# Neighbouring tokens on a partition in both q, k, v stages, and the expert choice packed by TensorE

## Time and profile before

| what | value |
|---|---|
| median of 3 runs | 3302.39 us (3301.63 to 3307.78) |
| profiled execution, its own time | 3321.07 us |
| span of the profiled execution | 3319.4 us |
| TensorE busy / VectorE / ScalarE / GpSimd | 86% / 66% / 48% / 22% |
| mean granted TensorE clock | 0.908 |
| DMA | 489.03 MB, 147 GB/s over the span |
| stages, us from the start | q, k, v 0; softmax attention 228; routing 1124; experts 1397; linear q, k, v 1722; linear attention 2010; last MLP 2335 |

### The profile page before, as it was taken

One profiled execution on the slowest core, in us unless ns is written; L12 is line 12 of the kernel. 1 busy time (PEld: TensorE's weight loads), 2 busy tenths in 40 slices (PEclk: granted clock), 3 DMA queues, 4 the chain that ended last, 5 costly groups with the idle time before them and its releaser, 6 DMA issues. The chain is left out here.

```text
span 3319.4 us, 59131 instructions
## 1 busy us (share of the span) xinstructions
PE 2858.0 (86%) x19969; PEld 2057.9 (62%) x19969; DVE 2207.0 (66%) x6121; ACT 1602.5 (48%) x2398; POOL 730.4 (22%) x877
## 2 busy tenths in 40 slices
PE   7849999999999577578856777999399999999998
PEld 6734444444444266467755564556288888888887
DVE  5548999999999278593327773434466666666664
ACT  3313777777777444343315553445244444444443
POOL 0021222222222133236754431222000000000000
PEclk9877999999999766689988997889699999999999
DMA  7996656666664278647868986543343434333241
GB/s 199 254 200 90 115 112 105 111 113 112 114 112 84 89 251 288 213 159 205 220 163 249 299 267 221 172 152 114 126 110 81 96 96 89 102 82 109 74 98 45
DMA packets 429959, 489.03 MB, mean 147 GB/s; under 512 B 92880, under 2 KB 310000, under 8 KB 429552
## 3 DMA queue, kind: packets, MB, share of 16 engines
q1 hardware_dynamic: 419072, 470.52, 55.3%
q0 software_dynamic: 10240, 14.16, 2.4%
q10 hardware_dynamic: 496, 2.42, 0.3%
HBM read 280.34 MB, written 206.10 MB: 147 GB/s over the span
## 5 line engine op out<-in xcount | busy, mean ns | idle before, releaser
L545 ACT ACTIVATE att_pr<-att_e_ps 128x1024 f32<-128x1024 f32 (+2 forms) x640 | 567.2, 938 | 202.2 <-PE att_e_ps L597 202.2
L573 PE MATMUL att_m_ps<-att_ks,att_qs 63*128 63x512 f32 (+3 forms) x1536 | 465.7, 433 | 46.7 <-PEq L39 38.3
L507 DVE CUSTOM_DVE_ANT_0 att_kept<-att_m_ps,att_causal 128x256 f32<-128x256 f32 (+3 forms) x1024 | 448.5, 488 | 47.9 <-DVEq L39 21.9
L573 PEld LDWEIGHTS att_m_ps<-att_ks,att_qs 63*128 63x128 f32 x1536 | 234.1, 189 | 376.8 <-DVE att_mx L510 148.4
L510 DVE TENSOR_REDUCE att_mx<-att_m_ps 128x1 f32<-128x512 f32 x512 | 323.4, 684 | 21.4 <-PE att_m_ps L573 17.4
L486 POOL TENSOR_SCALAR_AFFINE_SELECT att_pr<-att_pr 128x256 f32<-128x256 f32 (+1 forms) x384 | 181.2, 484 | 695.8 <-PEq L588 692.2
L617 PE MATMUL att_o_ps<-att_pr,att_vs 128*32 128x512 f32 (+3 forms) x3072 | 328.9, 501 | 3.0 <-ACT att_pr L545 1.6
L2587 ACT ACTIVATE fin_hh<-fin_hid 128x512 fp32r<-128x512 f32 x192 | 121.4, 632 | 397.9 <-DVE fin_hid L2433 300.0
L597 PE MATMUL att_e_ps<-att_qs,att_ks 64*128 64x512 f32 (+3 forms) x1536 | 269.2, 376 | 5.8 <-ACT att_pr L545 3.2
L2326 POOL TENSOR_TENSOR fin_rs<-fin_ve,fin_mhalf 128x4 f32<-128x4 f32 x48 | 48.4, 1007 | 927.5 <-POOLq L39 927.5
L2429 DVE TENSOR_TENSOR fin_hid<-fin_gate,fin_u_ps 128x512 f32<-128x512 f32 x192 | 131.7, 686 | 136.4 <-ACT fin_gate L2581 82.6
(11 more groups left out here) (332 smaller groups left out, 6905.0 us busy)
## 6 DMA issues: line engine op xcount, KB each, us to landing
fin_raw<-weights SPq DMA_DIRECT2D x32, 1024.0 KB, 14.1
att_qs<-q_high SPq DMA_DIRECT2D x128, 128.0 KB, 5.0
att_ks<-k_high SPq DMA_DIRECT2D x128, 128.0 KB, 6.6
attended<-att_ot SPq DMA_DIRECT2D x64, 256.0 KB
acc<-att_zero SPq DMA_DIRECT2D x64, 256.0 KB, 2.2
moe_w<-w SPq DMA_DIRECT2D x128, 128.0 KB
lqk_a<-acc SPq DMA_DIRECT2D x32, 512.0 KB
attended<-lin_ot SPq DMA_DIRECT2D x32, 512.0 KB, 3.5
```

The costliest lines, as they stand in the source:

```text
L507: e.tensor_tensor_reduce(kept[:, n % MBUF, 0:w], m_ps[:, n % MBUF, 0:w], causal[:, BLK - w:], 1.0, -3e38, ALU.add, ALU.max, mx[:, h, at, q ...
L545: e.activation(out, src, ACT.Exp).then_inc(exp_done, 1)
L573: e.matmul(m_ps[:, (2 * i + n) % MBUF, 0:w], qs[rows, j, p, q * P:(q + 1) * P], ks[rows, j, p, h * BLK:h * BLK + w], start=True, stop=True ...
```

## The change

In both q, k, v stages, four neighbouring tokens lie on one partition: token 4p + t of the block is on partition p at place t. A partition's part of a load or store is then one piece (x 4 KB, v of softmax attention 1088 B, v of linear attention 2176 B, rows of k 2 KB). The columns of the transposed x come in the order t, p; q and k (and the features, in the linear stage) are put back in order of tokens as they are read from PSUM, with a step of 128 elements between neighbours. v's copy in the first stage is made in four instructions, v's sum in the linear stage in two, and their DMAs are joined to one. The transposes of k read its features at a step of four elements. What lies in DRAM is as before.

In the routing stage, the four transposes are replaced by four products of the mask with a 128x32 matrix `digits` of 8, 4, 2, 1, made by GpSimd at the start of the stage: the result holds for each expert and four neighbouring tokens one number. `chosen` is 64 by 2048. In the expert stage the three packing steps of VectorE go, `pack` stands ahead of the first `split`, and SyncE waits for the choice and the first weight before it issues the second weight and the second block, and for the first block before the experts' weights.

```diff
@@ phase_qkv
-        vo = ph.sb("vo", [P, 2, TPB, NH, VW])
+        vo = ph.sb("vo", [P, 2, NG, TPB, GH * VW])
-        x_v = x_d.rearrange("(b j t p) c -> b j p t c", j=2, t=TPB, p=P)
-        v_v = v_d.rearrange("(b g j t p) c -> b j t p g c", b=B, g=NG, j=2, t=TPB, p=P)
+        x_v = x_d.rearrange("(b j p t) c -> b j p (t c)", j=2, t=TPB, p=P)
+        v_v = v_d.rearrange("(b g j p t) c -> b j p g (t c)", b=B, g=NG, j=2, t=TPB, p=P)
+        def in_order(a):
+            return a.rearrange("p (t q) -> p q t", t=TPB)
-                        for t in range(TPB):
-                            e.dma_start(v_v[b[0], j, t], vo[:, j, t].rearrange("p (g h) d -> p g (h d)", g=NG)
-                                        ).then_inc(stored[j], 16)
+                        e.dma_start(v_v[b[0], j], vo[:, j].rearrange("p g t c -> p g (t c)")).then_inc(stored[j], 16)
-                            e.tensor_tensor(ol[:, j, c], qk[:, c], oh[:, j, c].bitcast(fp32),
+                            e.tensor_tensor(ol[:, j, c].rearrange("p (q t) -> p q t", t=TPB), in_order(qk[:, c]),
+                                            oh[:, j, c].bitcast(fp32).rearrange("p (q t) -> p q t", t=TPB),
-                            e.activation(oh[:, j, c], qk[:, c], ACT.Copy).then_inc(oh_ready, 1)
+                            e.activation(oh[:, j, c].rearrange("p (q t) -> p q t", t=TPB), in_order(qk[:, c]), ACT.Copy).then_inc(oh_ready, 1)
-                        e.activation(vo[:, j, :, :, 0:HD], vp[:].rearrange("p t (h d) -> p t h d", d=HD), ACT.Copy
-                                     ).then_inc(vo_ready, 1)
+                        for t in range(TPB):
+                            i = e.activation(vo[:, j, :, t].rearrange("p g (h d) -> p g h d", d=VW)[:, :, :, 0:HD],
+                                             vp[:, t].rearrange("p (g h d) -> p g h d", g=NG, d=HD), ACT.Copy)
+                        i.then_inc(vo_ready, 1)
@@ phase_project_route
-        rt = ph.sb("rt", [E, 2, BLK])
+        rt = ph.sb("rt", [E, 2, BLK // PACK])
+                step(e.memset(digits[:], 0.0))
+                for n in range(PACK):
+                    step(e.affine_select(out=digits[:], in_=digits[:], compare_op=ALU.not_equal,
+                                         fill=float(2 ** (PACK - 1 - n)), base=-n, pattern=[[-PACK, P // PACK]],
+                                         channel_multiplier=1))
-                            i = e.transpose(r_ps[:, t * P:(t + 1) * P], mask[:, t], ident[:])
+                            cols = slice(t * (P // PACK), (t + 1) * (P // PACK))
+                            i = e.matmul(r_ps[:, cols], mask[:, t], digits[:], start=True, stop=True)
@@ phase_shared_and_experts
                 load(0)
+                e.wait_ge(choice_loaded, 32)
+                e.wait_ge(w_loaded[0], 16)
                 e.dma_start(w2f[:], s2_d).then_inc(w_loaded[1], 16)
                 load(1)
+                e.wait_ge(loaded[0], 32)
                 for n in range(SETS):
                     load_experts(n)
-                    member = chosen[:].rearrange("p (g i) -> p g i", i=PACK)
-                    step(e.scalar_tensor_tensor(bits[:], member[:, :, 0], 2.0, member[:, :, 1], ALU.mult, ALU.add))
-                    for i in range(2, PACK):
-                        step(e.scalar_tensor_tensor(bits[:], bits[:], 2.0, member[:, :, i], ALU.mult, ALU.add))
-                split(0, w1h, w1l, w1f)
                 e.wait_ge(choice_loaded, 32)
                 e.wait_ge(iotas_ready, 2)
                 pack()
+                split(0, w1h, w1l, w1f)
                 split(1, w2h, w2l, w2f)
-                    e.dma_start(chosen[i * E0:(i + 1) * E0], mt_d[:, i * HALF:(i + 1) * HALF]).then_inc(choice_loaded, 16)
+                    e.dma_start(bits[i * E0:(i + 1) * E0], mt_d[:, i * GROUPS:(i + 1) * GROUPS]).then_inc(choice_loaded, 16)
@@ phase_linear_qkv
-            return d.rearrange("(b j t p) c -> b j p t c", j=2, t=TPB, p=P)
+            return d.rearrange("(b j p t) c -> b j p (t c)", j=2, t=TPB, p=P)
-        kt_v = fkt_d.rearrange("(b f j t p) c -> b j f p t c", b=B, f=2, j=2, t=TPB)
-        v_v = v_d.rearrange("(b f j t p) c -> b j f p t c", b=B, f=2, j=2, t=TPB)
+        kt_v = fkt_d.rearrange("(b f j p t) c -> b j p f (t c)", b=B, f=2, j=2, t=TPB)
+        v_v = v_d.rearrange("(b f j p t) c -> b j p f (t c)", b=B, f=2, j=2, t=TPB)
-                                e.scalar_tensor_tensor(phi[:, j, k], qk[:, k], bqk1[:, k:k + 1], ex[:, k], ALU.add,
-                                                       ALU.max).then_inc(phi_done, 1)
+                                e.scalar_tensor_tensor(phi[:, j, k].rearrange("p (q t) -> p q t", t=TPB),
+                                                       in_order(qk[:, k]), bqk1[:, k:k + 1], in_order(ex[:, k]),
+                                                       ALU.add, ALU.max).then_inc(phi_done, 1)
-                        e.tensor_tensor(vo[:, j, :, :, 0:HD], vp[:].rearrange("p t (h d) -> p t h d", d=HD),
+                        for f in range(2):
+                            cols = slice(f * P, (f + 1) * P)
+                            i = e.tensor_tensor(vo[:, j, f].rearrange("p t (h d) -> p t h d", d=VW)[:, :, :, 0:HD],
...
-                                                phi[:, c[1], 2 + f, t * P:(t + 1) * P], ident[:])
+                                                phi[:, c[1], 2 + f].rearrange("p (q t) -> p t q", t=TPB)[:, t], ident[:])
```

More of the change, by code:

```diff
@@ L28 @@
 XW = C + E0
+PACK = 4
+WORD = 2 ** PACK
 EPS = 1e-5
@@ L180, in _ @@
                 e.sem_inc(pe_consts, 1)
-                step(e.memset(vo[:].rearrange("p j t h d -> p (j t h) d")[:, :, HD:VW], 1.0))
+                step(e.memset(vo[:].rearrange("p j g t (h d) -> p (j g t h) d", d=VW)[:, :, HD:VW], 1.0))
                 e.sem_inc(ones_ready, 1)
@@ L792, in phase_project_route @@
         ssum = ph.sb("ssum", [P, TPB])
-        rt = ph.sb("rt", [E, 2, BLK])
+        rt = ph.sb("rt", [E, 2, BLK // PACK])
+        digits = ph.sb("digits", [P, P // PACK])
         t_ps = ph.ps("t_ps", [P, KC, BLK])
@@ L1196, in phase_shared_and_experts @@
         zero = ph.sb("zero", [DUMMY, XW])
-        chosen = ph.sb("chosen", [P, HALF])
         bits = ph.sb("bits", [P, GROUPS])
@@ L1656, in _ @@
                 e.sem_inc(pe_consts, 1)
[L1657 removed]
+                step(e.memset(vo[:].rearrange("p j f t (h d) -> p (j f t h) d", d=VW)[:, :, HD:VW], 1.0))
                 e.sem_inc(ones_ready, 1)
@@ L2733, in build @@
     rows = dram("expert_rows", N + DUMMY, XW)
-    chosen = dram("chosen", E0, N)
+    chosen = dram("chosen", E0, N // PACK)
     shared = dram("shared", N, C)
```

40 lines of the change are left out of this document (20 added, 20 removed).

## The result

| | us | ratio to before, 95% interval |
|---|---|---|
| predicted | 3253 (3205 to 3280) | 0.9850 |
| before, timed beside it, median of 4 | 3305.09 (3301.63 to 3318.15) | |
| after, median of 4 | 3258.89 (3255.69 to 3263.04) | 0.9836 [0.9814, 0.9858] |
| after, in a second set of runs (before: 3317.13, median of 17), median of 5 | 3257.44 (3250.84 to 3264.90) | 0.9832 [0.9812, 0.9852] |
| after, span of the profiled execution | 3256.8 | |

The change makes the kernel 1.6% faster, and the predicted time lies 6 us from the measured one. The ratio given is not the quotient of the two medians: that is 0.9860 in the first set and 0.9820 in the second, or 46 and 60 us.

A forecast was written before the change was run, and what follows sets the result against it. DMA queues, with v's 272 B pieces, bound the first stage; VectorE's token list the experts; DMA and VectorE both the linear q, k, v stage. -30 + 0 - 13.5 - 5 = -48.5 us from 3302.4: about 3253 us, range 3205 to 3280.

The forecast's parts named there:

- part 1: Softmax q, k, v stage: larger pieces relieve DMA, VectorE comes next, period 12.09 to about 10.4 us; -30 us.
- part 4: Linear q, k, v stage: less DMA, more VectorE work, period near 16.0 us, start and tail shorter; -5 us.
- The price for a packet: DMA queues: 12 ns + 0.038 ns per byte from linear and routing stages; 39 ns per 272 B packet in first stage.
- That is 0.74 us per 1024, so 0.37 us per 512. I take this price: First stage: VectorE's stepped PSUM reads priced like the choice's stepped SBUF pack; four differences go from 2.50 to 3.98 us.
- Rival 1: Both q, k, v stages: steps on PSUM, or all steps, cost nothing; 3216 to 3238 us, chance 0.32.
- Part 2: Routing stage: four small products replace the transposes, at something like half their 1.06 us, off the chain; 0 us.
- Part 3: Expert stage: choice lands sooner, packing steps go, search for the largest starts 13.5 us earlier; -13.5 us.
- Rival 4: Expert stage: the late second weight holds VectorE before its search, the 13.5 us shrink to 3; 3264 us, chance 0.12.
- Start and tail carry stores and loads alone: -3 and -4: Linear q, k, v stage: its beginning and end save 3 and 4 us.
- because the accumulators arrive before it and GpSimd adds them then: 0.5 us: Linear q, k, v stage: VectorE's sum of x, 1.75 us at the median, 1.22 undisturbed, gives back 0.5 us.
- Rival 2: VectorE's differences and features: stepped reads cost three times per element, kernel slower by 36 us; 3338 us, chance 0.09.
- Rival 3: Packets cost by bytes alone: first stage keeps its 12.09 us period, linear stage gets no relief; about 3311 us, chance 0.05.

The follow-up runs named there:

- experiment 5: Changed kernel without SyncE's waits ahead of the second weight and the experts' weights in the expert stage: 3265.99 us, 0.9842 of the kernel before.
- exponential in order: Changed kernel, but ScalarE writes the linear stage's exponentials already in token order, so VectorE's feature steps only on PSUM: 3247.94 us (0.9785) and 3245.59 us (0.9794).
- experiment 4: Two kernels built on exponential in order: VectorE's scaling for x put first, 3260.96 us (0.9830); GpSimd's second accumulator sum left out, 3225.89 us (0.9738).

## Why the prediction was right

The largest term, the first stage, had its bound right and its size wrong, and the small miss of the total is in part luck: an error of 17 us in part 1 and one of 13 us in part 4 had opposite signs.

**What bounds the kernel now**: right for the first stage. The 272 B pieces of v held it, shown by putting them back alone. The price for a packet (12 ns + 0.038 ns per byte, 39 ns for 272 B), fitted on two other stages, gave 141 us of engine time per block for the change, measured 142.

**Part 1** failed by its size: -30 forecast, -47 measured, 46 to 50 by undoing it. The step that failed is "That is 0.74 us per 1024, so 0.37 us per 512. I take this price": it carried the price of a stepped read of SBUF over to PSUM. The measured price is 684 - 687, nothing. With it the forecast's own lower end applies, "with free steps the period is 9.3 us and the stage gives 46 us". Rival 1's half on PSUM came true, 9.27 us, and with it the forecast of VectorE as what is late next was wrong: it is TensorE, whose rows at full clock were there to be read, 9.28 us for the undisturbed block. ScalarE's four copies of v cost nothing, as said. Of the 47 us, 39 came from the periods, where 24 were forecast, and 7 from the stretch behind the last copy, where 6 were. (That stretch's 178 us of engine time do not follow from the forecast's own prices, 92 + 80 = 172; it moves the forecast by 0.4 us.)

**Part 2** was right, 273.2 and 271.1 us against 272.3. But the four products with 32 columns are not "half" of the transposes: TensorE is busy with L1155 for 17.0 us, over 16 blocks 1.06 us each, the same as four transposes. Each product is two instructions (x128), each transpose was one. It lay under a wait, so the error cost nothing.

**Part 3** was right in mechanism and near in size: search 12.5 us sooner of 13.5; the choice used 8.8 us after the start, where the forecast put the landing at 6; wait for the list 6.0, not 8. The stage took 303.9 to 312.0 us in ten traces, against 325.7 and 322.6 with the old choice; in time, undoing it cost 16 us. SyncE's waits, which the forecast counted among the reasons, are worth nothing (experiment 5). Rival 4 (second weight late) has this much truth: 0.5 to 0.8 us. The list came 12.5 us sooner and the stage is 14 to 22 us shorter; where the rest comes from was not looked into.

**Part 4** failed in sign: -5 forecast, +8 measured. The stage of the changed kernel took 298.8 to 302.2 us in its seven traces, against 292.0 and 293.1 with the code of before. VectorE's added work was as forecast (+0.38 us per feature), and so was the period in the middle of the stage (16.1 us; the forecast's own terms, 15.86 + 1.65 - 1.4, give 16.1, though it wrote 16.0). Two other steps failed. They show when the stage is cut at ScalarE's first, third, fifteenth and last copy:

```profile
1757.39 1.00 ACT L1770 ACTIVATE lqk_xh<-lqk_t_ps 128x1024 fp32r<-128x1024 f32 x1
...
1785.90 1.01 ACT L1770 ACTIVATE lqk_xh<-lqk_t_ps 128x1024 fp32r<-128x1024 f32 x1
...
1976.83 1.01 ACT L1770 ACTIVATE lqk_xh<-lqk_t_ps 128x1024 fp32r<-128x1024 f32 x1
...
1988.44 1.02 ACT L1770 ACTIVATE lqk_xh<-lqk_t_ps 128x1024 fp32r<-128x1024 f32 x1
```

```profile
1695.55 1.00 ACT L1787 ACTIVATE lqk_xh<-lqk_t_ps 128x1024 fp32r<-128x1024 f32 x1
...
1728.73 1.01 ACT L1787 ACTIVATE lqk_xh<-lqk_t_ps 128x1024 fp32r<-128x1024 f32 x1
...
1921.90 1.01 ACT L1787 ACTIVATE lqk_xh<-lqk_t_ps 128x1024 fp32r<-128x1024 f32 x1
...
1935.25 1.02 ACT L1787 ACTIVATE lqk_xh<-lqk_t_ps 128x1024 fp32r<-128x1024 f32 x1
```

| us | before | linear stage of before | after | after |
|---|---|---|---|---|
| start to the first copy | 34.8 | 34.2 | 33.2 | 33.1 |
| first two periods | 28.5 | 28.1 | 33.2 | 32.4 |
| twelve periods | 190.9 | 193.7 | 193.2 | 195.2 |
| last period | 11.6 | 11.0 | 13.3 | 14.1 |
| last copy to the end | 26.2 | 26.2 | 27.1 | 27.0 |

The first failed step is "Start and tail carry stores and loads alone: -3 and -4": in the first trace they gave -1.6 and +0.9. The second is that the relief of the middle was taken for all sixteen blocks: the first two periods and the last one became 6.4 us longer, where the added 1.65 us of VectorE's work show in full (13.6 to 15.1 us for the first, 11.6 to 13.3 for the last; the second, 14.9 to 18.1, bears a sum of x of 3.11 us for 1.59 besides). These two make up the 13 us.

In the middle the sum came out with a wrong term in it. What was to be given back "because the accumulators arrive before it and GpSimd adds them then: 0.5 us" was not: the mean of the sum of x over the stage did not fall but rose, from 1.94 us (before) and 1.71 (the linear stage of before) to 2.19 and 2.14, and the sums of x still fall together with GpSimd's, the first of which waits 99 us over the stage for its loads. The other term, the wait for GpSimd's sum, was about right, 15 us over the stage for a forecast of 0.9 per block: 20.2 us before, and after

```profile
DVE lqk_st L745 <- POOL lqk_a L1678: 4.9, 1, 4.9
```

In all, VectorE's idle time fell from 3.2 us per period, over the twelve in the middle, to 1.7 and 2.0, so that its added work hardly made them longer. The DMA share of 0.97, read as a bound ("both matter"), was hardly one: with the features back at 746 ns it fell to 0.81, and the stage took 291.5 us against 293.1 with the small packets and no step.

**The rivals.** Rival 1 was half right (PSUM free, SBUF not); with PSUM free in part 1 the sum gives 3302.4 - 46 - 13.5 - 5 = 3238 us, a ratio of 0.9805, just outside the measured interval. The forecast came nearer by the luck named above. Rival 2 fell (684 ns, 1127 ns). Rival 3 fell, with the first stage at a period of 9.27.

**The two rules on stepped reads** each hold for one memory. The rule on lines of the Trainium skill ("SBUF — State Buffer", section on door 1, the DMA port swizzle) agrees with the trace for SBUF, 1127 against 747 ns. Of PSUM the Trainium skill says there that a non-contiguous access slows matmuls; the prediction carried this over to VectorE and ScalarE, where it doesn't hold: 684 against 687 and 598 against 600 ns. The Trainium skill's mode 1x ("VectorE: DVE Perf Modes", strides and PSUM operands work, at one result a cycle) agrees for the stepped PSUM operand and not for the stepped SBUF operand, where the measurement decides.

## What to carry to other kernels

When the pieces of a DMA are as small as the 272 B here, price the queue by the packet (39 ns for 272 B, 76 for 1685 B), and put the tokens on the partition so that the pieces grow; do the reordering where it is read from PSUM, on whichever engine reads it first, and write SBUF in order, since a step on PSUM cost nothing and one on SBUF half as much again. A busy DMA queue is a bound only if somebody waits for it last: take out a little work of each suspect before counting on relief, and look at a stage's first and last periods apart from its middle. Where VectorE adds two SBUF tensors beside GpSimd doing the same, look at the minimum beside the median of both: the difference is one engine standing still.

## What was not expected of the hardware

- A PSUM read at a step of 512 B cost nothing, for VectorE (684 against 687 ns) and ScalarE (598 against 600; the exponential 678 against 681). A step on an SBUF operand costs 0.38 us for 512 elements (1127 against 747), the same as the pack's 0.74 for 1024 at a step of 16 B.
- A stepped stationary operand loads more slowly. Weight loads of k's transposes at a step of 16 B (exponential in order), and without step (linear stage of before):

```profile
L1834 PEld LDWEIGHTS lqk_t_ps<-lqk_ident,lqk_phi 128*128 128x128 f32 x128 | 17.8, 212 | 41.1 <-DVE lqk_xl L1744 40.8 <-DVE lqk_phi L1729 0.3
```

```profile
L1824 PEld LDWEIGHTS lqk_t_ps<-lqk_ident,lqk_phi 128*128 128x128 f32 x128 | 16.3, 158 | 40.1 <-DVE lqk_xl L1735 39.8 <-DVE lqk_phi L1726 0.3
```

  212 against 158 ns, at granted clocks of 0.93 and 0.92. TensorE sat idle for some 40 us ahead of these loads in both, so it probably costs nothing; no run changed it alone.
- The recorded DMA share can pass 1.0 (1.08 with v in small pieces), so engine time divided by 16 overstated the period there, 12.1 us against 11.2.
- An unchanged stage, the linear attention, varied by 14 us between executions. The changed first stage repeats within 2 us (180.2 to 181.8), so each stage has its own grain, to be taken from several traces before a difference is read.
- Two sums that meet on VectorE and GpSimd don't share: the later one stands nearly still for all that is left of the earlier (experiment 4).
- A product of 64x128 by 128x32 keeps TensorE as busy as a transpose of the same mask with 128 columns, 1.06 us per four.
- One sum less on GpSimd raised TensorE's granted clock in the linear stage from 0.93 to 1.00, while its busy share went from 0.76 to 0.81.
